# First gather portion of a graph layer with an LSTM: each gather waits until TensorE's products are at most twelve tiles behind it

## The reference, cut to what matters

```python
def gnn(x, src, dst, w_e, W, b):              # x: 6250 x 256, 100000 edges
    support  = einsum('ni,oi->no', layernorm(x), W) + b
    messages = support[dst] * w_e[:, None]    # a gather of 256-wide rows
    return segment_sum(messages, src, 6250)   # added up by src row

x = x + gnn(...)
x = x + lstm_and_attention(layernorm(x))      # 256 wide LSTM over the rows, then sums
```

## Time and profile before

| | |
|---|---|
| median of 3 runs | 2006.28 us (1996.38, 2006.28, 2009.58) |
| the profiled execution | 1996.12 us, span of its instructions 1993.9 us |
| first portion (gathers 258.0 to 673.7 us) | 224 tiles, 26 chunks |
| second portion (gathers 680.9 to 1648 us) | 606 tiles |
| PE / DVE / ACT / POOL busy over the span | 77 / 67 / 28 / 57 % |

### The profile page before, as it was taken

One profiled execution on the slowest core, in us unless ns is written; L12 is line 12 of the kernel. 1 busy time (PEld: TensorE's weight loads), 2 busy tenths in 40 slices (PEclk: granted clock), 3 DMA queues, 4 the chain that ended last, 5 costly groups with the idle time before them and its releaser, 6 DMA issues.

```text
span 1993.9 us, 35190 instructions
## 1 busy us (share of the span) xinstructions
PE 1534.4 (77%) x9341; PEld 1310.0 (66%) x9341; DVE 1336.8 (67%) x3992; ACT 549.6 (28%) x1889; POOL 1141.2 (57%) x1191
## 2 busy tenths in 40 slices
PE   5778847677666658787788778778787878999993
PEld 2458736566555437676677667667676767899992
DVE  8999868878777545565556556556556655566665
ACT  0111100000000003232323223223223335777771
POOL 0319856656556665655656665665665650068884
PEclk8889957878887768898879888999978989999996
DMA  8101122224222333333334333333333333444444
GB/s 195 33 21 36 37 84 74 78 66 119 72 68 68 87 91 100 100 121 105 103 97 126 103 104 120 103 105 124 105 103 99 125 101 107 124 121 120 125 120 135
DMA packets 65050, 195.61 MB, mean 98 GB/s; under 512 B 21761, under 2 KB 23141, under 8 KB 64125
## 3 DMA queue, kind: packets, MB, share of 16 engines
q0 software_dynamic: 46096, 111.01, 20.1%
q1 hardware_dynamic: 18904, 84.00, 13.8%
HBM read 153.75 MB, written 41.04 MB: 98 GB/s over the span
## 4 chain that ended last, share of the span: by engine, by line
PE 43%; DVE 23%; issue 15%; another core or an unknown queue 9%; DVEq 6%; ACT 2%; POOL 1%; DMA 1%; ACTq 0%; SPq 0%; POOLq 0%
PE bank L1736 11%; PE bank L1704 9%; PE bank L1723 7%; PE bank L1661 5%; PE bank L1730 5%; DVE big_a L1069 4%; PE bank L1628 3%; DVE big_a L1065 2%; DVE big_b L1126 2%; DVE big_c L1120 2%; DVEq L1129 2%; DVE big_c L1067 1%; DVEq L1120 1%; DVE listed L1007 1%
## 5 line engine op out<-in xcount | busy, mean ns | idle before, releaser
L561 POOL DMA_INDIRECT big_a<-support_scratch,stg_g x606 | 583.5, 963 | 384.2 <-issue 156.7
L1126 DVE TENSOR_TENSOR big_b<-big_b,bank 125x256 f32 x830 | 346.3, 417 | 352.9 <-remote 192.0
L1704 PE MATMUL bank<-big_a,big_c 128*125 128x256 f32 x1212 | 395.4, 433 | 39.9 <-issue 18.5
L1120 DVE TENSOR_SCALAR big_c<-consts_sb,listed 128x125 f32<-128x125 f32 x830 | 296.0, 357 | 50.5 <-issue 33.0
L1723 PEld LDWEIGHTS bank<-xt,w_ih 128*128 128x128 f32 x1600 | 239.2, 216 | 105.1 <-issue 71.1
L1723 PE MATMUL bank<-xt,w_ih 128*128 128x125 f32 x1600 | 253.0, 303 | 68.9 <-issue 53.4
L515 POOL DMA_INDIRECT big_a<-support_scratch,stg_g x224 | 214.4, 957 | 152.4 <-ACT stg_g L643 91.5
L1704 PEld LDWEIGHTS bank<-big_a,big_c 128*125 128x125 f32 x1212 | 220.3, 215 | 75.4 <-issue 57.0
L1736 PE MATMUL bank<-big_c 128*128 128x125 f32 x2048 | 256.9, 280 | 5.0 <-DVE big_c L1279 5.0
L1730 PEld LDWEIGHTS bank<-big_c 128*128 128x128 f32 x1600 | 231.9, 212 | 40.3 <-ACT bank L697 24.9
L1736 PEld LDWEIGHTS bank<-big_c 128*128 128x128 f32 x2048 | 241.3, 191 | 15.8 <-issue 7.5
(11 more groups left out here) (260 smaller groups left out, 1897.0 us busy)
## 6 DMA issues: line engine op xcount, KB each, us to landing
big_c<-gate_input_scratch SPq DMA_DIRECT2D x64, 508.0 KB, 3.5
gate_input_scratch<-pr SPq DMA_DIRECT2D x25, 1016.0 KB
big_a<-support_scratch,stg_g POOLq DMA_INDIRECT x830
support_scratch<-pr SPq DMA_DIRECT2D x12, 448.0 KB
big_b<-in_x SPq DMA_DIRECT2D x2, 1904.0 KB
out<-big_a SPq DMA_DIRECT2D x2, 1456.0 KB
big_b<-in_x SPq DMA_DIRECT2D x1, 1792.0 KB
out<-big_a SPq DMA_DIRECT2D x1, 1344.0 KB
```

Source lines behind the costliest of these rows:

```text
L561: pool.indirect_dma_start(out=ring[:, s, :], out_offset=None, in_=sup_d, in_offset=bass.IndirectOffsetOnAxis(ap=stg_g[:, q, n:n + 1], axis ...
L1120: V.tensor_scalar(oneh[:, s % HOTS, 0:SEGS], iota[:, 0:SEGS], src_of[:, ds(t, 1)], w_of[:, ds(t, 1)], ALU.is_equal, ALU.mult).then_inc(oh_ ...
L1126: V.tensor_tensor(at, at, bank[4 + s % PSR][0:SEGS, 0:D], ALU.add).then_inc(added, 1)
L1704: mm(bank[4 + s % PSR][0:SEGS, 0:D], oneh[:, s % HOTS, 0:SEGS], ring[:, s, :], start=True, stop=True).then_inc(prod, 1)
```

## The change

A wait for `prod` and an increment of a semaphore of its own (`go`, which nobody waits for) are put ahead of each gather of the first portion. `at_tile * HALF` is the first tile T of the half-round, so the wait ahead of the gather of tile T + j is for T + j - 12 finished products. ScalarE's copy already stands for T - 8 of them. The new wait thus asks for nothing more at j = 0 to 4, and for one, two and three more products at j = 5, 6 and 7.

```diff
+LOOK_1 = 12
...
                 pool.sem_inc(go, 1)
                 for j in range(count):
                     s = (first + q * HALF + j) % RING
+                    pool.wait_ge(prod, at_tile * HALF + (RING + j - LOOK_1))
+                    pool.sem_inc(go, 1)
                     pool.indirect_dma_start(
                         out=ring[:, s, :], out_offset=None, in_=sup_d,
                         in_offset=bass.IndirectOffsetOnAxis(ap=stg_g[:, q, j:j + 1], axis=0)).then_inc(gat[s], 16)
```

## The result

The changed kernel takes **1974.95 us** (median of four runs, 1971.56 to 1979.11) against 2003.6 us before (four runs, 1996.38 to 2009.58): a ratio of 0.9859, 95% interval 0.9818 to 0.9901. The forecast was 1984 us.

The account below looks back on a forecast made before the run. No engine is full; TensorE's products reach VectorE's additions late during GpSimd's runs of transfers. Stops gain 13 x 1.7 = 22 us, all else 0: 2006.3 - 22 = 1984 us, range 1960 to 2020.

Parts of the forecast that it names:

- products handed over late in runs of transfers: First portion: TensorE's products reach VectorE late during GpSimd's indirect transfers, most of 79.5 us idle before additions.
- the length of 2.5 us in the rule: Products come late once a transfer run has lasted some 2.5 us, then all at once 0.8 to 1.9 us after it.
- Added instructions: 0.: 224 waits with increments in GpSimd's list between gathers: taken as 0, upper bound 67 us of GpSimd's time, mostly hidden.
- The wait stops GpSimd "in most half-rounds": Wait at j = 5 to 7: GpSimd stops after five gathers, cutting the run of eight into five and three.
- Idle ahead of additions to about 55 us.: Profile sign in the first portion: VectorE's idle time before additions falls from 79.5 to about 55 us.
- The "1.5 us lost": Half-rounds with scatters: GpSimd's later end pushes the next gathers deeper into the next additions, up to 1.5 us lost.
- 13 x 1.7 = 22 us.: First portion's gain: 1.7 us for each of 13 half-round pairs, chosen between bounds of -1.2 and 6.1 us.
- Second portion unchanged: The second portion and everything behind it only start earlier, with the same length.
- No change: Rival: gathers don't make products late, or the wait doesn't cut the run; 2006 us (1996 to 2012), chance 0.30.
- Slower, by a stop that moves the run: Rival at gathers j = 5 to 7 and following scatters: products held until all transfers end; 2030 us, chance 0.14.
- Much faster: Rival: nearly all products get through, 13 pairs x 5 us = 65 us; 1941 us (1930 to 1958), chance 0.10.
- the sum would be 0: By the skill's rule late products have another cause, so the gain is 0 instead of 22 us; the first rival.

Follow-up runs that it names:

- experiment 1: The changed kernel with waits for fifteen instead of twelve tiles, so always met: 1701.8 and 1700.46 us, ratios 1.0007 and 0.9998 to the kernel before, products on time.
- experiment 5: The changed kernel itself timed again beside the kernel before, in a session with late products: 2000.03 us against 2022.99, ratio 0.9875.
- experiment 4: Kernel before, plus the sixth gather waiting until the fifth's rows landed: 1762.28 and 1762.7 us on time (1.0362, 1.0361); 1984.99 us late (0.9823).
- experiment 2: The changed kernel with only the sixth gather (j == 5) of a half-round waiting: 1700.43 us, ratio 0.9992 to the kernel before, products on time.
- experiment 7: The kernel before with first-portion gathers of 512 instead of 1024 bytes a row: 1699.58 us, ratio 0.9994, products on time.
- experiments 1 to 3: The third is the changed kernel with a tighter wait, LOOK_1 = 8 instead of 12: 1703.49 us, ratio 1.0012 to the kernel before, products on time.

## Why the prediction was right, step by step

- *What bounds: products handed over late in runs of transfers*. It held, in late sessions. The always-met kernel, with products on time, has 9.1 us of such waits (experiment 1), so the 79.5 us were a hold and not work. What did not hold is the length of 2.5 us in the rule: additions were prompt 15 us into a run of the changed kernel itself, and late ones are frequent only beyond 10 us. The window on whose edge the prediction put the eighth product is not of that size.
- *Added instructions: 0.* Right: ratios 1.0007 and 0.9998 on time; gathers still 954 ns, gaps still 0.30 us.
- *The wait stops GpSimd "in most half-rounds".* Half right. Followed along the 28 half-rounds of the changed kernel, the sixth gather has more than 0.9 us of idle time ahead of it in 13, nearly every other one, and in a further two single gathers stop for 0.4 to 1.2 us. The other thirteen runs are whole, and some join the next one to thirteen in a row. But the stops are up to 6.3 us long where I had put 2.3.
- *Idle ahead of additions to about 55 us.* It fell to 42.6, more than forecast. The mis-sized part: I had counted 24.5 us of relief and no new wait; there were 36.9 us, and 18.8 us came back ahead of the builds, for chunk products held by the same kind of run. The step left out the builds. The "1.5 us lost" by a run pushed into the next additions stood in for it, and was by its size about right (18.8 / 13 = 1.4 us a pair). The net, 18.1 us for 22, is thus near by two misses that run against each other. In the profile of experiment 5 the relief was 15.7 us and 4.6 came back.
- *13 x 1.7 = 22 us.* Measured: the last gather of the portion 19.9 us earlier; the profiled execution 1996.12 to 1979.11, 17 us; medians 2003.6 to 1974.95, 28.7 us, interval of the ratio 20 to 36 us. By the additions of the earlier trace rows a pair now takes (619.38 - 335.68) / 10 = 28.4 us, for which I had named 28.2; in experiment 5 it is 29.0. The 1.7 us a pair were a choice between the bounds of -1.2 and 6.1 us. That it came out so near is in part luck; what the record bears out is the sign, the place and that stops make the gain; that they make it by shorter runs it does not bear out (experiment 4).
- *Second portion unchanged:* right (974.5 and 976.4 us from portion end to last gather).
- *The rivals.* No change: it would have left 79.5 us and did not come in a late session, but in an on-time one it is what experiment 2 shows for the one wait. Slower, by a stop that moves the run: not for the change; the landing stop shows the mechanism's price, +62 us, where GpSimd is the bound. Much faster: the additions did get nearly that much relief in single half-rounds (4.5 us instead of 9.5), but half of the total was handed to the builds.
- *The rule of the Trainium skill* ("SBUF — State Buffer", "Who interferes with whom": PE and ACT never wait on anyone). The on-time sessions agree with it: additions 0.62 us apart through whole runs. In the late ones TensorE's matmuls come 2.1 us apart during gathers, and a kernel takes 1984.99 us that takes 1762.28 elsewhere. The section is about the engines' ports to SBUF, and no run here shows that the hold is one at a port, so the rule isn't refuted as it stands. What failed is the step from it to "the sum would be 0": TensorE's results can be late beside gathers all the same. What makes a session late no run here shows.

**What stays open.** What differs between late and on-time sessions: outside the two gather portions nothing moved (first gather at 258.0 and 257.7 us, 335.8 and 335.6 us from the last addition to the end), and chip 5 was seen both ways four minutes apart, so it isn't the chip. Whether bytes, descriptors or GpSimd's issuing hold the products in a late session: experiment 7 fell into an on-time one. Whether a stop helps by shortening a run or by moving it off the additions. That the change costs nothing on time was not measured for it as a whole, only for its `j == 5` wait, for a looser and for a tighter constant (experiments 1 to 3).

## What to carry to other kernels

When an engine's results are picked up late in long runs of another engine and come through soon after the run ends, try a stop in that run or move it off the place where they are picked up, and tie it to the progress of the one that waits: such a stop vanishes by itself when nothing is late, while a fixed one cost 3.6% there. A wait removed ahead of one consumer may come back ahead of the next (here additions, then builds), so list every consumer of the late engine before pricing. And take a rule found in one execution as a rule of that execution until the kernel before has been seen in another session.

## What the runs showed of the hardware

- One and the same kernel took 1700.7 and 1700.8 us in two sessions and 2003.6 to 2023.0 us in the five others (medians). The difference lies in the portions in which GpSimd gathers: 332.5 against 414.8 us (always-met waits on time, before late) and 761 against 966 us (598.2 to 1359.4; 680.9 to 1647.3). The gathers themselves take 958 and 957 ns.
- In late sessions what is held is not VectorE but what TensorE hands over, tile products and, as far as the builds' waits tell, chunk products alike. Held back for 4 and 7 us, the tile products come through within 2 us of the run's end.
- The hold goes one way, as far as the kernel before shows it. In the earlier trace rows the addition at 517.07 waits 2.28 us for a product; TensorE's next product, which needs the bank that this addition frees at 517.49, starts 0.15 us later:

```profile
517.64 0.68 PE L1661 MATMUL bank<-big_a,big_c 128*125 128x256 f32 x2 [2.41 <-issue]
```

- With one stop of 2.6 us in every eight gathers a late session cost the first portion nothing: 395.7 us, 395.6 on time (experiment 4), with runs of transfers as long as before.
- A wait that is already fulfilled ahead of an indirect transfer costs nothing: the gap is 0.30 us with it and without it, and 224 added waits with their increments moved the time of an on-time session's run by at most 0.16%.
